# Later weight requests, a value matrix in one piece and a quantised matrix cast on GpSimd: a change to the first chunks of an attention-and-gate kernel

## The chip, the cores and the metric

The kernel runs on the 8 cores of one Trainium2 chip. Each core gets two of the 16 sequences and its own copy of the weights; the cores exchange nothing. The metric is the device time of the slowest core, in microseconds (us), as a median of 3 runs. A profile of one execution, taken on the slowest core, goes with it.

## What is computed

Per core x is 4096 x 1024 in float32. The reference, cut to what matters:

```python
xn = _layernorm(x, axis=-1)
q, k, v = xn @ Wq.T, xn @ Wk.T, xn @ Wv.T       # 16 heads of 64
scores = q k^T / 8, each query sees itself and the 127 keys before it
s = softmax(scores) @ v @ Wo.T
q_lhs = round(xn / (max|xn| per row / 127)); q_rhs = round(rhs / (max|rhs| per column / 127))
g = silu((q_lhs @ q_rhs) * lhs_scale * rhs_scale)
x + s * g
```

## The kernel before, in words

The 4096 rows are cut into 32 chunks of 128 rows. Names: `xs` (four buffers) holds a chunk of x as it lands, `xnr` its normalised bf16 form and `xnt` its transpose; `qlr` and `qlt` are the same for the quantised rows. `qrhs` is the quantised right-hand matrix, `rsb` its column scales. `wq`, `wk`, `wv`, `wo` are the weights in bf16, each asked for as 8 row blocks, which GpSimd's DMA queue casts from float32 on the way (`load_w`). rhs comes from SyncE's queue in 8 blocks (`load_rh`, called rh0 to rh7 here).

Every engine has its program written out by hand, and waits on counters of the others. PE's order is `pe_order`: a list of groups. TX, TL, TR, TA are transposes on PE (of `xnr`, `qlr`, of a cast rhs block, of the attention output); Q, K, V, O are the projections; F is the quantised product; RS spreads the column scales over the partitions; S and A are scores and attention-times-V of a quarter of the heads. A group name has an index (chunk, pair of chunks or block) and a half. `slot_gaps(c)` gives the groups that PE does between the four score blocks b = 0 to 3 of chunk c; "slot (c,b)" below is the stretch after score block b of chunk c. VectorE and ScalarE walk the same list: `evac_v` and `evac_a` empty the PSUM banks, in the order of the slots, and the table `extra` puts other work into a slot. A PSUM bank is filled again four groups later, so a late evacuation stops PE.

The start-up before chunk 0 runs: x of chunks 0 to 3 arrives; VectorE takes mean and variance (`bn`), GpSimd the reciprocal root (`rstd`), VectorE writes `xnr` (`xn`), PE transposes it (TX). ScalarE centres (`cen`) and scales (`qp`), VectorE takes the row maximum (`amax`) and finishes the quantised row (`ql`). PE does Q, K and V of chunks 0 to 3, then TL, TR 0 to 3 and RS. A rhs block goes through five steps: `rabs` (VectorE, maximum of the block), `rscale` (VectorE, once for two blocks), `rq` (ScalarE, scale and round), `rcast` (GpSimd, to bf16), TR (PE). In the steps of V the eight row blocks of `wv` are consumed in the order in which they arrive: first blocks 0 to 3 for all eight groups, then blocks 4 to 7 group by group. The gate of chunk c is `zev` (VectorE, F out of PSUM), tanh (`th`, ScalarE), `gate` (VectorE).

SyncE asks for x of chunks 0 to 3 at once, for rh0 to rh3 when block 4 of `wk` has landed, for x 4 and 5 when block 2 of `wv` has, and for rh4 to rh7 and x 6 when block 6 has. GpSimd asks for `wv` when rh1 has landed.

## Time and profile before

| | |
|---|---|
| median of 3 runs | 712.0 us (710.03 to 713.23) |
| the profiled execution | 712.11 us |
| its span on the slowest core | 710.5 us (the cores: 703.9 to 710.5 us) |
| PE busy | 665.4 us, 94% of the span |
| VectorE / ScalarE / GpSimd busy | 67% / 49% / 24% |
| granted TensorE clock, mean of the core | 0.985 |

The span runs from the first to the last instruction of that core; 1.6 us of the execution's time lie around it. Busy PE is not PE at its peak: a wait shows as idle time, and a low clock as longer busy time. The granted clock of a stretch is a share of full speed, 1.00 being 2.4 GHz and 0.50 being 1.2 GHz.

### The profile page before, as it was taken

To read this page: it belongs to the slowest core of one execution; us is meant where nothing else is said; L and a number is where in the kernel's file an instruction comes from. 1 tells how busy PE (TensorE), PEld (TensorE's weight loads), DVE (VectorE), ACT (ScalarE), POOL (GpSimd) and SP (SyncE) were. 2 spreads that over 40 slices of the span, in tenths; PEclk is the share of its full clock that TensorE was granted. 3 is DMA by queue.
4 is the path that set the end of the run, shared out by engine and by line. 5 is a ranking of instruction groups with operands and counts; after the bars stand their busy time and mean duration, and the time that the engine had idled before them with its cause. 6 is when DMAs were issued, how large, how long until landed. Compare 5 with 4: busy or idle time off the path is not lost.

```text
span 710.5 us, 17009 instructions; the slowest of 8 cores (703.9 to 710.5 us)
## 1 busy us (share of the span) xinstructions
PE 665.4 (94%) x5724; PEld 413.0 (58%) x5724; DVE 475.9 (67%) x958; ACT 346.7 (49%) x473; POOL 172.6 (24%) x281
## 2 busy tenths in 40 slices
...
GB/s 191 149 200 188 182 18 76 149 119 134 134 129 127 119 88 97 131 120 134 134 120 127 115 102 94 130 120 134 135 122 125 115 92 104 131 89 76 76 90 149
DMA packets 109859, 86.40 MB, mean 122 GB/s; under 512 B 92112, under 2 KB 92240, under 8 KB 109776
## 3 DMA queue, kind: packets, MB, share of 16 engines
...
q8 instruction: 49, 0.80, 0.5%
...
## 4 chain that ended last, share of the span: by engine, by line
PE 87%; DVE 5%; DMA 4%; issue 2%; POOL 1%; ACT 1%; DVEq 0%; SPq 0%; ACTq 0%; POOLq 0%
PE pj L675 44%; PE pj L666 29%; PE psc L759 5%; PE pav L783 4%; PE pav L785 2%; DMA xs<-x 2%; DMA wv<-wvt 2%; DVE ee L356 1%; PE pav L666 1%; PE psc L666 1%; DVE sm L326 1%; DVE gg L385 0%; DVE sm L291 0%; DVE sm L403 0%; POOL aot L831 0%
## 5 line engine op out<-in xcount | busy, mean ns | idle before, releaser
L573 ACT ACTIVATE ee<-psc 128x1024 bf16<-128x1024 f32 (+1 forms) x128 | 128.4, 1003 | 157.8 <-PE psc L759 152.9
L825 POOL TENSOR_TENSOR xr<-tt,xr 128x512 f32<-128x512 f32 x63 | 80.4, 1277 | 370.0 <-DVE tt L391 344.6
L675 PE MATMUL pj<-wv,xnt 128*128 128x512 bf16 x480 | 118.7, 391 | 5.1 <-DMA wv<-wvt 3.8
L675 PE MATMUL pj<-qrhs,qlt 128*128 128x512 bf16 x512 | 122.0, 382 | 0.0
L675 PE MATMUL pj<-wo,aot 128*128 128x512 bf16 x512 | 116.4, 379 | 1.2 <-ACT aot L313 1.2
L666 PE MATMUL pj<-xnt,wq 128*128 128x256 bf16 x960 | 112.3, 276 | 1.9 <-DVE xnt L311 1.8
L666 PE MATMUL pj<-xnt,wk 128*128 128x256 bf16 x960 | 109.7, 273 | 0.0
L356 DVE TENSOR_TENSOR ee<-ee,mask_s 128x1024 bf16<-128x1024 bf16 (+1 forms) x128 | 104.1, 813 | 7.6 <-ACT ee L573 2.1
L666 PEld LDWEIGHTS pj<-xnt,wq 128*128 128x128 bf16 x960 | 93.1, 99 | 13.5 <-issue 2.1
L666 PEld LDWEIGHTS pj<-xnt,wk 128*128 128x128 bf16 x960 | 92.0, 98 | 10.3
L675 PEld LDWEIGHTS pj<-wo,aot 128*128 128x128 bf16 x512 | 49.5, 98 | 60.0 <-issue 1.7
L391 DVE TENSOR_TENSOR tt<-pj,gg 128x512 f32<-128x512 f32 x64 | 44.0, 690 | 54.4 <-PE pj L675 53.4
L675 PEld LDWEIGHTS pj<-qrhs,qlt 128*128 128x128 bf16 x512 | 48.3, 99 | 54.3 <-issue 2.8
L675 PEld LDWEIGHTS pj<-wv,xnt 128*128 128x128 bf16 x480 | 45.9, 100 | 53.1 <-issue 12.0
L539 ACT ACTIVATE xs<-xs,sm 128x1024 f32<-128x1024 f32 x32 | 36.6, 1148 | 75.5 <-DVE xnr L321 75.5
L367 DVE TENSOR_TENSOR ao<-pav,sm 128x256 bf16<-128x256 f32 x128 | 54.4, 425 | 13.3
L326 DVE TENSOR_REDUCE sm<-xs 128x1 f32<-128x1024 f32 x32 | 39.0, 1218 | 34.9 <-ACT xs L539 34.9
L759 PEld LDWEIGHTS psc<-qt,kt 64*128 64x128 bf16 x992 | 28.1, 94 | 49.6 <-issue 49.4
L378 DVE SCALAR_TENSOR_TENSOR zz<-pj,sm,rsb 128x512 f32<-128x512 f32 x64 | 47.8, 747 | 10.7 <-PE pj L675 7.8
L759 PE MATMUL psc<-qt,kt 64*128 64x128 bf16 x992 | 50.1, 219 | 2.5 <-ACT ee L573 2.5
L783 PE MATMUL pav<-vv,ee 128*128 128x65 bf16 x480 | 46.5, 196 | 6.0 <-DVE ee L356 3.4
L556 ACT CAST kt<-pj 128x512 bf16<-128x512 f32 x60 | 33.6, 582 | 32.2 <-PE pj L666 32.2
...
## 6 DMA issues: line engine op xcount, KB each, us to landing
...
```

The source lines that it names most:

```text
L326: op(lambda: v.reduce_max(col(c, AMAX), xs[c % XS][:], AX.X, apply_absolute_value=True), "v")
L356: op(lambda: v.tensor_tensor(a, a, m, ALU.mult), "v", ("mask", c, b))
L367: op(lambda: v.tensor_tensor(view(ao[c % 2], b * 256, (64, 4), (1, 64)), view(p, 0, (66, 4), (1, 64)), bass.AP(sm, C_RS + 4 * (b % 2), [[1 ...
L378: op(lambda: v.scalar_tensor_tensor(zz[h], banks[bank["F", c, h]], col(c, LSH), rsb[:, h * 512:(h + 1) * 512], ALU.mult, ALU.mult), "v", ( ...
L391: op(lambda: v.tensor_tensor(tt[h], banks[bank["O", c, h]], gg[c % 2][:, h * 512:(h + 1) * 512], ALU.mult), "v", ("ev", "O", c, h))
L539: op(lambda: a.activation(xs[c % XS][:], xs[c % XS][:], AF.Identity, scale=-1.0, bias=col(c, MEAN)), "a", ("cen", c))
L573: op(lambda: a.activation(o, i, AF.Exp, scale=0.125), "a", ("exp", c, b))
L666: yield [(lambda kc=kc, m=m: t.matmul(p[:, m * 256:(m + 1) * 256], w[:, kc * 1024 + (2 * j + m) * 128:kc * 1024 + (2 * j + m + 1) * 128], ...
L675: yield [lambda kc=kc: t.matmul(p[:], src[:, off + kc * step:off + kc * step + 128], w[:, kc * 1024 + j * 512:kc * 1024 + (j + 1) * 512], ...
L759: todo.append(lambda m=m, kk=kk, ko=ko, rows=rows, q0=q0: t.matmul(psc[:, q0:q0 + 128], kk[rows, m * 256 + ko:m * 256 + ko + 128], qt[s % ...
L783: todo.append(lambda out=out, e0=e0, vp=vp: t.matmul(out, e[:, e0:e0 + 128], vp, start=True, stop=False))
L825: op(lambda: p.tensor_tensor(r, tt[h], r, ALU.add), "p", ("add", c, h))
```

## The change

Six edits. GpSimd asks for the first block of `wq` only when the statistics of chunk 0 are done; the remaining requests follow in other portions. All 8 blocks of `wv` are asked for in one go, ahead of the casts of rhs blocks 0 to 3; SyncE asks for x 4 and 5 behind block 6 of `wv`. Blocks 4 to 7 of rhs are scaled and rounded on GpSimd (`rq_p`) and not on ScalarE, and two blocks of `wo` go ahead of them, six in between. ScalarE empties both halves of TX and TR from index 4 on. The orders of the start-up and of chunks 0 to 3 change on every engine: F of chunks 0 and 1 stands in the slots of chunk 0, TX 4 and 5 at the end of chunk 0, and VectorE's work on chunks 4 and 5 and on rhs 4 to 7 behind the first mask. In chunks 2 and 3 SyncE's transposes stand ahead of its stores. At the end the last transpose stands between the two halves of the last O.

```diff
@@ slot_gaps
     if c == 0:
-        return [halves("TX", 4, 5), halves("V", 4)[:1], halves("V", 4)[1:], []]
+        return [[("F", 0, 0)], [("F", 1, 0)] + halves("TR", 4), halves("TR", 5), halves("TX", 4, 5)]
     if c == 1:
-        v, f1 = halves("V", 5), [("F", i, 1) for i in range(2)]
-        return [halves("TR", 4, 5), v[:1] + halves("TR", 6, 7), v[1:] + [("RS", 0, 1)] + f1[:1], f1[1:]]
+        v4, v5 = [[g] for g in halves("V", 4)], [[g] for g in halves("V", 5)]
+        return [v4[0] + halves("TR", 6, 7), v4[1] + [("RS", 0, 1)], v5[0] + [("F", 0, 1)], v5[1] + [("F", 1, 1)]]
@@ pe_order
-    out = one(halves("TX", 0, 1)) + [("G", q0, range(4))] + one(halves("TX", 2)) + [("G", q0, range(4, 5))]
-    out += one(halves("TX", 3)) + [("G", q1, range(5)), ("G", q0, range(5, 6)), ("G", q1, range(5, 6))]
+    out = one(halves("TX", 0, 1)) + [("G", q0, range(6))] + one(halves("TX", 2, 3)) + [("G", q1, range(6))]
...
-    out += one(halves("TL", 2, 3) + halves("TR", 0, 1, 2, 3) + [("RS", 0, 0), ("F", 0, 0), ("F", 1, 0)])
+    out += one(halves("TL", 2, 3) + halves("TR", 0, 1, 2, 3) + [("RS", 0, 0)])
...
-    out += [("G", [g], range(6)) for g in last] + one([("TA", NC - 1, 3)])
+    out += [("G", last[:1], range(6))] + one([("TA", NC - 1, 3)]) + [("G", last[1:], range(6))]
     out += [("G", [g], range(6, 8)) for g in last]
@@ evacuator
+    if k in ("TX", "TR") and i >= 4:
+        return "a"
@@ emit_sync
-            landed(sync, "wv2", 0)
+            landed(sync, "wv6", 0)
             load_x(sync, 4)
             load_x(sync, 5)
-            landed(sync, "wv6", 0)
             for i in range(4, 8):
                 load_rh(sync, i)
...
-                if c >= 2:
+                if c in (2, 3):
+                    t_ql(sync, c + 2)
+                elif c >= 4:
                     store(sync, c - 2)
...
+                if c in (2, 3):
+                    store(sync, c - 2)
@@ emit_vector
             evac_v(v, ("TX", 0, 0))
+            evac_v(v, ("TX", 1, 0))
             bn(v, 3)
-            evac_v(v, ("TX", 1, 0))
...
+            extra = {(0, 0): [(bn, 4), (bn, 5), (rabs, 4), (rabs, 5), (rscale, 4)], (0, 1): [(rabs, 6)], (0, 2): [(xn, 4), (xn, 5)],
+                     (0, 3): [(rabs, 7), (rscale, 6)], (1, 0): [(rdiag, 1)], (1, 2): [(amax, 4)],
+                     (2, 0): [(ql, 4)], (2, 2): [(amax, 5)], (3, 0): [(ql, 5)]}
@@ emit_scalar
-            extra = {(0, 1): [(rq, 6)], (0, 2): [(rq, 7)], (1, 0): [(qp, 4)], (1, 3): [(qp, 5)]}
+            extra = {(1, 0): [(cen, 4)], (1, 2): [(cen, 5)],
+                     (1, 3): [(qp, 4)], (2, 3): [(qp, 5)]}
@@ GpSimd
+        def rq_p(p, i):
+            need(p, "v", ("rsc", i - i % 2))
+            st = stage[i]
+            op(lambda: p.tensor_scalar(st[:], st[:], sm[:, C_RSC + i:C_RSC + i + 1], MAGIC, ALU.mult, ALU.add),
+               "p", ("rq", i))
@@ emit_gpsimd
+            need(p, "v", ("bn", 0))
             load_w(p, 0, range(2))
-            need(p, "v", ("bn", 0))
-            load_w(p, 0, range(2, 4))
             rstd(p, 0)
-            load_w(p, 0, range(4, 8))
+            load_w(p, 0, range(2, 6))
             rstd(p, 2)
+            load_w(p, 0, range(6, 8))
             load_w(p, 1, range(8))
             landed(p, "rh1", 0)
-            load_w(p, 2, range(4))
-            rcast(p, 0)
-            rcast(p, 1)
-            load_w(p, 2, range(4, 8))
-            rcast(p, 2)
-            rcast(p, 3)
+            load_w(p, 2, range(8))
+            for i in range(4):
+                rcast(p, i)
+            landed(p, "rh4", 0)
+            load_w(p, 3, range(2))
+            for i in (4, 5):
+                rq_p(p, i)
+                rcast(p, i)
             rstd(p, 4)
-            landed(p, "rh6", 0)
-            load_w(p, 3, range(8))
-            for i in range(4, 8):
+            load_w(p, 3, range(2, 8))
+            for i in (6, 7):
+                rq_p(p, i)
                 rcast(p, i)
```

GpSimd's queue from the second block of `wv` on (L831 and L828 are `rcast`, L818 is `rq_p`; `sm` rows are `rstd`). Before:

```order
L837 DMA wv<-wvt 128x1024 x3
L831 TENSOR_SCALAR aot<-gg 128x1024 [waits s_a] x2
L837 DMA wv<-wvt 128x1024 x4
L831 TENSOR_SCALAR ao<-zz 128x1024 [waits s_a]
L831 TENSOR_SCALAR ao<-tt 128x1024 [waits s_a]
L808 TENSOR_SCALAR sm<-sm 128x2 [waits s_v]
L810 TENSOR_TENSOR sm<-sm 128x2 [waits s_p]
L812 TENSOR_TENSOR sm<-sm 128x2 [waits s_p]
L814 TENSOR_TENSOR sm<-sm 128x2 [waits s_p]
L816 TENSOR_SCALAR sm<-sm 128x2 [waits s_p]
L818 TENSOR_TENSOR sm<-sm 128x2 [waits s_p]
L837 DMA wo<-wot 128x1024 [waits s_rh6]
```

With the change:

```order
L834 DMA wv<-wvt 128x1024 x7
L828 TENSOR_SCALAR aot<-gg 128x1024 [waits s_a] x2
L828 TENSOR_SCALAR ao<-zz 128x1024 [waits s_a]
L828 TENSOR_SCALAR ao<-tt 128x1024 [waits s_a]
L834 DMA wo<-wot 128x1024 [waits s_rh4]
L834 DMA wo<-wot 128x1024
L818 TENSOR_SCALAR xr<-xr,sm 128x1024 [waits s_v]
L828 TENSOR_SCALAR aot<-xr 128x1024 [waits s_p,s_t]
L818 TENSOR_SCALAR xr<-xr,sm 128x1024 [waits s_v]
L828 TENSOR_SCALAR aot<-xr 128x1024 [waits s_p,s_t]
L796 TENSOR_SCALAR sm<-sm 128x2 [waits s_v]
L798 TENSOR_TENSOR sm<-sm 128x2 [waits s_p]
```

The requests for `wv` stand together, and the requests for `wo` are split around two pairs of `rq_p` and `rcast`; `rstd` of chunks 4 and 5 has moved behind them.

VectorE behind the evacuation of TR 0 to 3 (L403 and L407 are `rabs`, the four short rows behind two of them `rscale`). Before:

```order
L321 TENSOR_SCALAR xnr<-xs,sm 128x1024 [waits s_p,s_t] x2
L403 TENSOR_REDUCE sm<-xr 128x1 [waits s_rh4]
L378 SCALAR_TENSOR_TENSOR zz<-pj,sm,rsb 128x512 [waits s_t,s_a,s_p]
L403 TENSOR_REDUCE sm<-xr 128x1 [waits s_rh5]
L409 TENSOR_SCALAR sm<-sm 128x2 [waits s_v]
L411 RECIPROCAL sm<-sm 128x2 [waits s_v]
L412 TENSOR_SCALAR sm<-sm 128x2
L414 TENSOR_SCALAR sm<-sm 128x2 [waits s_v]
L385 SCALAR_TENSOR_TENSOR gg<-gg,zz 128x512 [waits s_a]
L378 SCALAR_TENSOR_TENSOR zz<-pj,sm,rsb 128x512 [waits s_t,s_v]
L403 TENSOR_REDUCE sm<-xr 128x1 [waits s_rh6]
L385 SCALAR_TENSOR_TENSOR gg<-gg,zz 128x512 [waits s_a]
```

With the change (`rscale`'s last row and `zz`, the evacuation of F of chunk 0, come next):

```order
L360 TENSOR_TENSOR ee<-ee,mask_s 128x4x128 [waits s_a,s_lm]
L295 BN_STATS sm<-xs 128x6 [waits s_lx0]
L295 BN_STATS sm<-xs 128x6
L297 BN_AGGR sm<-sm 128x2 [waits s_v]
L295 BN_STATS sm<-xs 128x6 [waits s_lx1]
L295 BN_STATS sm<-xs 128x6
L297 BN_AGGR sm<-sm 128x2 [waits s_v]
L407 TENSOR_REDUCE sm<-xr 128x1 [waits s_rh4]
L407 TENSOR_REDUCE sm<-xr 128x1 [waits s_rh5]
L413 TENSOR_SCALAR sm<-sm 128x2 [waits s_v]
L415 RECIPROCAL sm<-sm 128x2 [waits s_v]
L416 TENSOR_SCALAR sm<-sm 128x2
```

The mask of the first score block stands first, and the statistics of chunks 4 and 5 and two block maxima lie between it and the first `zz`.

PE at the same place, behind RS (`qrhs,qlt` is F, `qt,kt` S, `vv,ee` A, `ident_s,xnr` TX and `ident_s,aot` TR). Before:

```order
L675 MATMUL pj<-qrhs,qlt 128x512 [waits s_a,s_v]
L675 MATMUL pj<-qrhs,qlt 128x512 x7
L675 MATMUL pj<-qrhs,qlt 128x512 [waits s_a,s_v]
L675 MATMUL pj<-qrhs,qlt 128x512 x7
L759 MATMUL psc<-qt,kt 128x128 [waits s_a,s_v]
L759 MATMUL psc<-qt,kt 128x128 x3
L660 MATMUL pj<-ident_s,xnr 128x128 [waits s_a,s_v]
L660 MATMUL pj<-ident_s,xnr 128x128 x3
L660 MATMUL pj<-ident_s,xnr 128x128 [waits s_a]
L660 MATMUL pj<-ident_s,xnr 128x128 x3
L660 MATMUL pj<-ident_s,xnr 128x128 [waits s_v]
```

With the change:

```order
L747 MATMUL psc<-qt,kt 128x128 [waits s_a,s_v]
L747 MATMUL psc<-qt,kt 128x128 x3
L663 MATMUL pj<-qrhs,qlt 128x512 [waits s_a,s_v]
L663 MATMUL pj<-qrhs,qlt 128x512 x7
L747 MATMUL psc<-qt,kt 128x128 [waits s_a]
L747 MATMUL psc<-qt,kt 128x128 x3
L773 MATMUL pav<-vv,ee 128x65 [waits s_v,s_a]
L773 MATMUL pav<-vv,ee 128x65 x3
L663 MATMUL pj<-qrhs,qlt 128x512 [waits s_a,s_v]
L663 MATMUL pj<-qrhs,qlt 128x512 x7
L648 MATMUL pj<-ident_s,aot 128x128 [waits s_a,s_p]
```

The first score block has moved ahead of F, and TR 4 stands where TX 4 and 5 stood.

## Rows read from the trace of the kernel before

**Rows 1.** Busy time in stretches: us, each engine's busy (instructions), granted clock, DMA share, GB/s.

```profile
20.00:38.00 18.00, 15.74 (x138) 13.37 (x137) 10.14 (x26) 8.01 (x11) 5.47 (x10) 1.00 1.04 153
64.30:71.50 7.20, 5.88 (x15) 2.03 (x16) 1.49 (x3) 1.74 (x3) 1.69 (x6) 0.53 0.82 211
230.00:650.00 420.00, 420.00 (x3663) 261.68 (x3662) 291.46 (x580) 213.95 (x293) 98.84 (x162) 1.00 0.54 117
```

**Rows 2.** Waits of PE: what waited for whom, us in total, times, longest.

```profile
PE pj L660 <- DVE xnr L321: 14.9, 1, 14.9
PE pj L660 <- DVE zz L378: 4.6, 1, 4.6
PE pj L675 <- DMA wv<-wvt: 3.8, 3, 2.5
PE pav L783 <- DVE ee L356: 3.4, 4, 1.3
```

**Rows 3.** Timeline of PE: start, us, operation, out<-in, count, idle before and releaser.

```profile
18.63 5.88 PE L666 MATMUL pj<-xnt,wq 128*128 128x256 bf16 x32 [1.85 <-DVE xnt L311]
...
28.53 0.60 PE L666 MATMUL pav<-xnt,wq 128*128 128x256 bf16 x4 [2.25 <-DVE xnt L311]
...
54.34 3.80 PE L675 MATMUL pj<-wv,xnt 128*128 128x512 bf16 x16 [1.17 <-DVE qlt L311]
...
66.79 5.04 PE L675 MATMUL pj<-wv,xnt 128*128 128x512 bf16 x13 [0.66 <-DMA wv<-wvt]
...
79.80 3.62 PE L675 MATMUL pj<-qrhs,qlt 128*128 128x512 bf16 x16
...
91.58 3.51 PE L675 MATMUL pj<-wv,xnt 128*128 128x512 bf16 x8
...
115.94 0.40 PE L759 MATMUL psc<-qt,kt 64*128 64x128 bf16 x8
```

**Rows 4.** Timeline of all engines, 0 to 30 us.

```profile
5.03 1.29 DVE L291 BATCH_NORM_STATS2 sm<-xs 128x6 f32<-128x512 f32 x2 [3.21 <-DMA xs<-x]
...
12.30 0.20 POOL L818 TENSOR_TENSOR sm<-sm 128x2 f32<-128x2 f32 x1
...
16.46 1.28 DVE L291 BATCH_NORM_STATS2 sm<-xs 128x6 f32<-128x512 f32 x2 [0.43 <-DMA xs<-x]
...
24.84 0.42 DVE L311 COPY xnt<-pav 128x512 bf16<-128x512 bf16 x1 [2.46 <-PE pav L660]
```

**Rows 5.** Timeline of all engines, 43 to 66 us.

```profile
43.59 2.11 POOL L837 DMA_DIRECT2D wv<-wvt  x4 [17.61 <-DMA gg<-rhst]
...
52.68 2.35 POOL L837 DMA_DIRECT2D wv<-wvt  x4
...
65.47 0.80 SPq L252 DMA_DIRECT2D xr<-rhst  x2
```

**Rows 6.** Timeline of all engines, 79 to 93 us.

```profile
80.05 0.59 ACT L589 COPY rsb<-pav 128x512 f32<-128x512 f32 x1 [0.47 <-PE pav L655]
...
82.61 1.21 DVE L403 TENSOR_REDUCE sm<-xr 128x1 f32<-128x1024 f32 x1
...
84.75 0.17 DVE L414 TENSOR_SCALAR sm<-sm 128x2 f32<-128x2 f32 x1
...
86.38 1.04 POOL L831 TENSOR_SCALAR aot<-xr 128x1024 bf16<-128x1024 f32 x1 [7.42 <-ACT xr L550]
...
86.79 1.18 DVE L385 SCALAR_TENSOR_TENSOR gg<-gg,zz 128x512 f32<-128x512 f32 x1 [1.87 <-ACT gg L579]
...
90.88 0.62 ACT L573 ACTIVATE ee<-psc 128x512 bf16<-128x512 f32 x1
```

**Rows 7.** Timeline of all engines, 699 to 711 us.

```profile
700.04 1.26 POOL L825 TENSOR_TENSOR xr<-tt,xr 128x512 f32<-128x512 f32 x1 [1.29 <-DVE tt L391]
...
700.67 2.75 PE L675 MATMUL pj<-wo,aot 128*128 128x512 bf16 x12 [0.61 <-ACT aot L313]
...
704.14 1.02 PE L675 MATMUL pj<-wo,aot 128*128 128x512 bf16 x4 [0.61 <-ACT aot L313]
```

27 lines of the change are left out of this document (5 added, 22 removed).

## The prediction

> **What bounds the kernel now.** I read the busy time in stretches first. From 230 to 650 us PE is busy for 420.00 of 420.00 us at full clock [rows 1], and the change touches nothing there; so only the ends can give time. The waits of PE come next: 14.9 us until the first normalised chunk, 4.6 us for a bank that `zz` had not left, 3.8 us for blocks of `wv`, 3.4 us for masks [rows 2]. In the timeline of PE [rows 3] the reader is to see a ladder of starts: Q at 18.63, the second Q half at 28.53, V at 54.34, the last 29 V products from 66.79, F at 79.80, V of chunk 4 at 91.58 and the first score block of chunk 2 at 115.94. I follow the change to that last mark and carry the difference over, since PE alone sets the pace behind it. A 512-column product takes 0.22 us (16 in 3.62 us from 79.80, less the 0.16 us that the last one outlasts its slot), twice that at the half clock (8 in 3.51 us from 91.58, granted clock 0.50 to 0.53 in such stretches [rows 1, 3]); a 256-column product takes 0.11 us. The sum is made against the profiled execution's 712.11 us, which is the median's 712.0 within 0.1.
>
> **First chunks.** Before, x of chunk 3 landed only at 16.46, because the `wq` blocks shared the DMA engines, and PE's first transpose waited for `xn` at 14.92, which stood behind the statistics of chunk 2 [rows 3, 4]. With the requests held back, statistics run without a pause: chunk 0 from 5.03 to 6.6, then 1.6 us each, so 8.2, 9.8. GpSimd's `rstd` ended 12.50 before, 2.7 us behind the statistics of chunk 1 [rows 4]: now 8.2 + 2.7 = 10.9. `xn` takes 0.8, so PE starts at 11.7, 3.2 us earlier. Q started 3.7 us after the first transpose before (14.92 to 18.63 [rows 3]), 0.5 of it behind the fourth chunk's statistics, which now come later, but ScalarE's copy, centring, copy keeps nearly all: 15.2.
> The first 32 Q products took 5.88 us, the start at low speed; then 16 more take 1.8: TX 2 and 3 start at 22.8 (before 24.3). What is late next is the second Q half: VectorE copies one transpose, does `ql` and `amax`, and copies the other; before, this ran from 24.84 until Q went on at 28.53, 3.7 us [rows 3, 4]. PE had 8 products to put under it, now none. Copy at 23.3, Q at 27.0, with PE idle for 3.1 us instead of 2.3. Then 80 Q products and not 88 (8.7 us) and 128 of K (14.0) lead to 49.7, TL and the wait behind it take 2.3 as before: V at 52.0, 2.3 us earlier than 54.34. The weights don't stop this: `wq` blocks 2 to 5 are asked for from 10.9 to 13.8, and a block moves in 1.7 us (0.262 MB at 153 GB/s, DMA share 1.04 [rows 1]), so block 5 is there at some 20, two steps ahead. The DMA engines are full in 20 to 38 us before; what x gains at the front the weights lose, so `wk` and rh1 land when they did, and `wv` is asked for at 43.6 as before [rows 5].
>
> **V.** Before, blocks 4 to 7 were asked for at 52.68, behind two casts that waited for ScalarE, and shared the engines with x 4 and 5, asked for at 52.72 when block 2 had landed [rows 5]; the last block let PE go on at 66.79, and the clock fell to 0.53 of full speed for 7 us [rows 1, 3]. Now all eight follow one another. Block 2 lands at 52.7 again and five more need 5 x 1.7 = 8.6: the last is there at 61.3. If the fourth block was already through by 53, it is 60.0; at 2 us a block, 62.7. Behind it stand 29 products, 6.3 us: V ends at 67.6 (bounds 66.3 and 69.0; PE alone, 52.0 + 64 x 0.22, asks for 65.9). Before it ended at 66.79 + 4.9 + 16 x 0.22 = 75.1. **Gain at this mark 7.5 us.** x 4 and 5 and rh4 to rh7 are asked for at some 60 instead of 52.7 and 65.5 [rows 5]: seven transfers of 512 KB, done by about 74, which the statistics of chunk 4 (67.6 + 7.2) just don't wait for. Casts 0 to 3 move behind the last `wv` request, at some 48, and are done by 59; TR needs them at 69. They cost nothing while V covers them.
>
> **Chunks 0 and 1**, counted from the end of V, T. TL, TR and RS take 4.7 (75.1 to 79.80 [rows 3]). The score block needs the bank of RS, which ScalarE emptied at 80.64, T+5.5 [rows 6]; F used to cover that wait, and PE now stands still for 0.9. Score block T+5.6, exponential 0.6 [rows 6], and 0.7 for the mask with its wake-up: T+7.2. Then VectorE does two statistics (3.1), two block maxima (1.2 each) and `rscale` (1.0, by 83.83 to 84.92 [rows 6]): T+13.6. GpSimd's `rq_p` is in no row. Its nearest is the cast of the same tile with one input, 1.04 us [rows 6]; the two-input addition of 512 columns, 1.26 [rows 7], would make it 2.5; ScalarE's loss of the work gives PE nothing. I take 1.04, since input and size are the cast's: TR 4 can start at T+13.6 + 0.1 + 1.04 + 0.15 + 1.04 = T+16.0. PE has F, S, A and F until T+9.8. **New wait 6.2 us**, and the clock will fall in it, as it did around the 4.6 us before. TR 5 follows at T+18.2; `rstd` of chunks 4 and 5 (2.5) and `xn` (0.8) come behind it, TX at T+21.7, masks and copies, V of chunk 4 at T+23.7. Before it was at T+16.5 (91.58), but with TR 4 and 5 and two F halves' worth of waits still ahead. At half clock V ends at T+27.2. GpSimd asks for six `wo` blocks (3.3), waits for `rscale` 6 (T+25.5) and does two pairs of 2.25: TR 6 T+28.0, TR 7 T+30.2. Behind them PE has 5 groups of 8 products (8.7), RS (0.9) and score work (1.7): T+42.0, and 0.6 for clock: T+42.6. Before it was 115.94 - 75.1 = T+40.8. **Loss 1.8 us.** The mark is at 67.6 + 42.6 = 110.2 instead of 115.9: 5.7 us earlier.
> One rule speaks against GpSimd here. The gate at 86.79 took 1.18 us and not the 0.68 of others of its kind beside the cast of 86.38 to 87.42 [rows 6]: it held back until the cast was through. The Trainium skill says the same in SBUF — State Buffer, Who interferes with whom: a VectorE instruction with two SBUF inputs and a GpSimd one that reads SBUF exclude each other for a whole instruction. By the row each of eight GpSimd steps can hold a mask or gate back by up to 1 us; nearly all of that lies while PE waits for the cast anyway. I count 0, upper bound 1.5.
>
> **Chunks 2 and 3, and the end.** The transposes ahead of the stores cost SyncE nothing that PE sees. `amax` 5 (2.1 us with its short steps) enters slot (2,2) and `ql` 5 slot (3,0); both lie under 3.5 us or more of products. The mask waits (3.4 us [rows 2]) fall mostly in chunk 3, behind `rstd` and centring, and stay: 0, bounds -3 and +1. At the end 12 O products, a transpose, a copy and 4 products ran from 700.67 to the last start at 704.14 and behind it [rows 7]; with the transpose between the halves, six products cover the copy, so the last four start at 703.4: gain 0.7.
> Sum: 712.1 - 5.7 - 0.7 = **705.7 us**.
>
> **The rivals.**
> (a) The new waits let the clock fall. PE idles 3.1 us ahead of Q, up to 2.5 in pieces in V, 6.2 in chunk 0. A fall at Q costs 4 us of work at half speed, 2 us; one in V another 2. For: behind the wait of 2.5 us for `wv` it stood at 0.53 [rows 1, 2]. Against: behind the 2.3 us ahead of 28.53 four products took 0.60, full speed [rows 3]. Time 709.5.
> The Trainium skill (TensorE: Matmul & The Clock Gate, What's actually happening) calls half speed the default that only activity lifts, which fits the slow first 32 Q products.
> (b) Slower: GpSimd becomes the bound of chunks 0 and 1. With `rq_p` at 2.5 us each pair takes 3.7 instead of 2.25: TR 5 and `rstd` 3.0 later, TR 7 4.5 later, 1.5 for the exclusions, 2 for clock: 713.7. It decides above about 4 us a pair, or 3.5 with low clock. Against: the cast's row.
> (c) More is won: the mask waits of chunk 3 go with the new order and the last `wv` block is there at 60: 701.7.
> (d) `wv` comes no sooner, since the DMA engines were full anyway. For: their share is near 1 throughout. Against: x 4 and 5 are 1 MB that now comes after. Time 709, with (a).
>
> **How the numbers follow.** The forecast 0.55 (703 to 708.3), (a) and (d) 0.23, (b) 0.07, (c) 0.15. A measurement of this kernel tells about 0.5%, 3.6 us, from no change. Faster than 708.4: the forecast and (c), 0.70; slower than 715.6: half of (b) and some for mechanisms unseen, 0.06; within: 0.24. The range reaches into (c) and over (a): 701.5 to 711.
>
> **What would show it.** PE's first transpose near 11.7 and V near 52; no wait for `wv` above 2 us and TL at 66 to 69; then the longest wait of PE behind the start at TR 4, some 6 us, released by GpSimd; `rq_p` near 1.04 us; chunk 2's first score block at 109 to 112. Wrong would be: `wv` landing after 64, PE at half clock for most of 27 to 52, or a pair on GpSimd above 3.5 us.

## The result

The changed kernel takes 714.8 us (median), the kernel before 712.0 us. The ratio is 1.0043, with a 95% interval of 1.0031 to 1.0056: the change makes this kernel slower by 0.4%, some 3 us, where 705.7 us and a gain of 6.3 us were forecast. The measured time also lies outside the range of 701.5 to 711.0 us. Single executions of either kernel were sometimes disturbed and much longer; the ratios leave these out.

The profiled execution of the changed kernel has its slowest core at 713.3 us. Spans and granted clock of the cores, then PE's waits on core 7, the slowest (what waited for whom, us in total, times, longest):

```profile
core 4: 713.2 us, clock 0.981
core 5: 711.4 us, clock 0.979
core 6: 709.5 us, clock 0.983
core 7: 713.3 us, clock 0.981
```

```profile
PE pj L648 <- DVE xnr L325: 18.7, 2, 16.9
PE pj L648 <- POOL aot L828: 9.6, 4, 5.8
PE pav L771 <- DVE ee L360: 4.4, 5, 1.3
PE pav L654 <- DVE xnt L315: 3.1, 1, 3.1
PE pj L654 <- ACT xnt L317: 1.5, 1, 1.5
```

Against [rows 2] the wait for `wv` (3.8 us) is gone: that part of the change does what it says. In its place stand 9.6 us behind GpSimd's casts (`aot`, L828) and 3.1 us instead of 2.3 ahead of the second Q half, and the first transpose is 2 us later (16.9 us on this core, 14.9 on the slowest one before). The ladder of PE's starts, to be laid beside [rows 3]:

```profile
20.23 6.87 PE L654 MATMUL pj<-xnt,wq 128*128 128x256 bf16 x48 [1.49 <-ACT xnt L317]
...
31.13 1.01 PE L654 MATMUL pav<-xnt,wq 128*128 128x256 bf16 x4 [3.14 <-DVE xnt L315]
...
58.87 3.37 PE L663 MATMUL pj<-wv,xnt 128*128 128x512 bf16 x14 [1.17 <-DVE qlt L315]
...
72.86 0.61 PE L648 MATMUL pav<-ident_s,qlr 128*128 128x128 bf16 x8
...
89.20 1.01 PE L648 MATMUL pj<-ident_s,aot 128*128 128x128 bf16 x8 [5.78 <-POOL aot L828]
...
98.31 3.60 PE L663 MATMUL pj<-wv,xnt 128*128 128x512 bf16 x8
...
118.59 0.40 PE L747 MATMUL psc<-qt,kt 64*128 64x128 bf16 x8
```

V ends at 72.86 (75.1 before), but the first score block of chunk 2 starts at 118.59 (115.94 before). Between the two the changed kernel spends 45.7 us and the kernel before 40.8. The clock says the same. Busy time in stretches of core 7 (columns as in [rows 1]):

```profile
26.00:40.00 14.00, 10.86 (x83) 8.52 (x81) 7.37 (x19) 4.33 (x6) 3.12 (x6) 0.76 1.07 152
58.90:72.90 14.00, 13.97 (x65) 6.29 (x66) 3.53 (x8) 6.32 (x9) 2.19 (x3) 1.00 0.82 217
85.00:95.00 10.00, 3.35 (x32) 2.29 (x32) 7.49 (x17) 4.42 (x8) 6.83 (x11) 0.66 0.00 1
95.00:105.00 10.00, 6.79 (x45) 3.76 (x46) 7.05 (x14) 5.68 (x9) 8.48 (x10) 0.66 0.77 115
150.00:160.00 10.00, 7.63 (x41) 3.30 (x40) 6.78 (x16) 3.77 (x5) 0.40 (x1) 0.83 0.33 91
```

V runs at full speed without a gap. From 85 to 95 us PE works for 3.35 of 10 us while VectorE and GpSimd are busy for 7.5 and 6.8: PE waits for their preparation, not for data (DMA share 0.00).

One core is not enough to read such small shifts, because the cores differ. The table gives medians over the eight cores of one profiled execution of each kernel: PE's first transpose, start of the second Q half, of K and of V, V's end (T), from there to V of chunk 4 and to the first score block of chunk 2 (S20), and from the first Q product in chunk 2 to the first in chunk 4 ("Q to Q", which holds chunks 2 and 3). All in us. The runs were made on several chips, on which the kernel before took 709.9 to 712.7 us; the ratio is always that of the times to the kernel before on the same chip, with its interval.

```
kernel            TX    Q2    K     V     T     T>V4  T>S20 Q to Q  ratio (interval)
before            15.2  28.1  39.1  55.4  74.3  16.5  40.8  39.1    1
after             14.1  29.7  40.1  56.4  70.5  25.5  46.8  41.6    1.0043 (1.0031 to 1.0056)
e1_early_w        15.3  30.2  40.5  56.8  70.7  25.5  46.9  41.5    1.0029 (1.0014 to 1.0044)
e2_late_w         14.1  27.1  37.7  54.0  75.4  16.5  40.8  39.0    1.0004 (0.9986 to 1.0022)
e3_rq_scalar      14.3  29.8  39.3  55.7  70.4  24.6  41.6  41.3    0.9961 (0.9944 to 0.9978)
e4_scales_first   14.6  30.0  40.4  56.6  70.7  20.0  40.4  41.5    0.9964 (0.9940 to 0.9987)
e5_start_order    14.1  27.6  37.3  53.5  69.2  25.5  45.9  41.4    1.0029 (1.0013 to 1.0045)
e6_wv_alone       15.7  28.9  39.6  55.8  69.8  21.9  46.7  39.0    1.0000 (0.9986 to 1.0013)
e7_e3_and_e4      14.0  29.3  38.9  55.3  70.0  20.3  37.2  40.5    0.9907 (0.9886 to 0.9928)
e8_rows45_early   14.2  29.4  39.5  55.7  69.7  25.5  45.9  39.1    1.0011 (1.0001 to 1.0021)
e9_four_parts     14.0  27.1  37.2  53.5  68.4  20.3  37.2  39.3    0.9889 (0.9868 to 0.9910)
e10_covers        14.4  27.1  37.7  54.0  68.8  20.4  37.8  37.0    0.9886 (0.9855 to 0.9918)
e11_five_parts    13.9  27.5  37.3  53.6  68.4  20.3  37.2  37.0    0.9852 (0.9829 to 0.9876)
e12_chunk3_alone  15.0  28.5  38.3  54.5  71.9  16.4  39.6  36.8    0.9966 (0.9955 to 0.9977)
```

The last row tells how well these marks repeat, since up to chunk 3 that kernel is the kernel before: its V ends at 71.9 us and not 74.3, and it needs 39.6 us and not 40.8 from T to S20, while T to V of chunk 4 agrees within 0.1. So a mark counted from the start of the program wanders by 2 to 3 us between two executions, and a stretch behind T by about 1.

By the first two rows the change wins 3.8 us at T (1.4 against the last row), loses 6.0 between T and S20, and loses another 2.5 in chunks 2 and 3. The end gives 0.6 us back: from the first Q of chunk 6 to the end of the span 513.03 us before (710.5 - 197.47, core 5) and 512.46 now (713.3 - 200.84, core 7).

### The profile page after: what moved, and what is told of

It is laid out like the page before. It is cut to its first block, busy times and chain, and to the rows that moved or that the text cites. A ratio compares the mean times of both kernels' runs of the same rounds, so it can differ in the third digit from the quotient of the medians.

```text
span 713.3 us, 17008 instructions; the slowest of 8 cores (709.2 to 713.3 us)
## 1 busy us (share of the span) xinstructions
PE 666.2 (93%) x5724; PEld 414.6 (58%) x5724; DVE 475.1 (67%) x952; ACT 346.2 (49%) x475; POOL 176.4 (25%) x285
## 4 chain that ended last, share of the span: by engine, by line
PE 85%; DVE 6%; issue 4%; POOL 2%; DMA 1%; ACT 1%; DVEq 0%; POOLq 0%; SPq 0%; ACTq 0%
PE pj L663 42%; PE pj L654 28%; PE psc L747 5%; PE pav L771 4%; PE pav L773 2%; DMA xs<-x 1%; DVE ee L360 1%; PE pav L654 1%; PE psc L654 1%; DVE sm L295 1%; DVE sm L330 1%; DVE sm L407 0%; DVE tt L395 0%; PE psc L663 0%; PE pav L663 0%
## 5 line engine op out<-in xcount | busy, mean ns | idle before, releaser
L663 PE MATMUL pj<-wv,xnt 128*128 128x512 bf16 x480 | 115.9, 386 | 1.2 <-DVE qlt L315 1.2
L360 DVE TENSOR_TENSOR ee<-ee,mask_s 128x1024 bf16<-128x1024 bf16 (+1 forms) x128 | 107.0, 836 | 9.2 <-ACT ee L566 4.1
L663 PEld LDWEIGHTS pj<-wv,xnt 128*128 128x128 bf16 x480 | 45.6, 99 | 46.8 <-issue 4.6
L549 ACT CAST qt<-pj 128x512 bf16<-128x512 f32 x60 | 33.4, 584 | 33.6 <-PE pj L654 33.6
```

The source lines that it names most:

```text
L360: op(lambda: v.tensor_tensor(a, a, m, ALU.mult), "v", ("mask", c, b))
L663: yield [lambda kc=kc: t.matmul(p[:], src[:, off + kc * step:off + kc * step + 128], w[:, kc * 1024 + j * 512:kc * 1024 + (j + 1) * 512], ...
```

## The experiments

**Are the late weight requests the cause?** The first run takes them back, the second makes them alone in the kernel before.

```diff
+            load_w(p, 0, range(2))
             need(p, "v", ("bn", 0))
-            load_w(p, 0, range(2))
+            load_w(p, 0, range(2, 4))
             rstd(p, 0)
-            load_w(p, 0, range(2, 6))
+            load_w(p, 0, range(4, 8))
             rstd(p, 2)
-            load_w(p, 0, range(6, 8))
```

> The changed kernel with one part undone: GpSimd asks for the blocks of wq as the kernel before did (blocks 0 and 1 at once, 2 and 3 behind the statistics of chunk 0, 4 to 7 behind the first rstd). All else stays. Theory: the late requests idle the DMA engines for some 5 us at the front, which is paid back as late wk and rh1, a late wv request (43 to 49.5 us over the cores) and a start of V at 54.6 to 58.9 us; and they carry the spread of x's arrival through to the end. Then V starts at 53.5 to 55.5 on all cores, the first score block of chunk 2 moves from 115.1 to 118.6 us down to 114 to 116, and the time falls by 2 to 3.5 us below the changed kernel's 714.8: 711.3 to 712.8, ratio to the kernel before about 1.000. Rival (the wait of 3.1 us ahead of the second Q half and its low clock set V's start, whenever the blocks come): V at 54.6 to 58 as now, time within 1 us of 714.8.

> The kernel before with one part of the change alone: the late requests for wq (nothing before the statistics of chunk 0, then 2 blocks, rstd, 4 blocks, rstd, 2 blocks). Theory (late requests cost on the slowest core): PE's first transpose 1 to 2 us earlier, the wv request up to 4 us later on the cores where x comes late, V starting at 55 to 58.5, time 2 to 3 us above the kernel before: ratio 1.003 to 1.004. Rival (the start of V is bounded by PE's own work, as the prediction had it): V 1 to 2 us earlier, ratio 0.997 to 0.999.

My theory fell in both. With the early requests the changed kernel starts V at 56.8 us as with the late ones (56.4), and its time is the same within the two intervals. In the kernel before, the late requests go with a V that starts 1.4 us earlier (55.4 to 54.0), as the rival said, though 54.5 was also seen without them (e12); but `wv` is then asked for at 46.3 us instead of 43.5 (medians of the cores), V ends at 75.4 instead of 74.3, and the ratio is 1.0004. No gain or loss of the requests shows in the time either way: what x gains, the last weights lose.

**What does PE wait for in chunk 0?** Two runs on two suspects, each a part of the new order. In the first, ScalarE scales and rounds blocks 4 to 7 again:

```diff
-            extra = {(1, 0): [(cen, 4)], (1, 2): [(cen, 5)],
+            extra = {(1, 0): [(rq, 6), (rq, 7), (cen, 4)], (1, 2): [(cen, 5)],
...
                     ex(a, c, b)
+                    if (c, b) == (0, 1):
+                        rq(a, 4)
+                        rq(a, 5)
...
             for i in (4, 5):
-                rq_p(p, i)
                 rcast(p, i)
```

> The changed kernel with scale-and-round of rhs 4 to 7 back on ScalarE (4 and 5 behind the second exponential, 6 and 7 behind the first of chunk 1); places on the other engines unchanged. Theory (GpSimd's pair of steps is on the path: 1.11 to 1.80 us each on four blocks, PE waits behind TR 4, TR 5 and TR 7): TR 4 within 0.3 us of where it is, TR 5 and V of chunk 4 2 to 2.5 us earlier, TR 7 2 us earlier, time 3 to 4 us below 714.8. Rival (VectorE's chain of statistics, maxima and scales behind the first mask is what PE waits for, GpSimd's steps are a small part): time within 1.5 us of 714.8, since TR 4 stays and ScalarE's exponentials and tanh come up to 1 us later.

In the second, VectorE takes the maxima of rhs 4 and 5 before the first mask:

```diff
             for i in range(4):
                 evac_v(v, ("TR", i, 0))
-            extra = {(0, 0): [(bn, 4), (bn, 5), (rabs, 4), (rabs, 5), (rscale, 4)], (0, 1): [(rabs, 6)], (0, 2): [(xn, 4), (xn, 5)],
+            rabs(v, 4)
+            rabs(v, 5)
+            rscale(v, 4)
+            extra = {(0, 0): [(bn, 4), (bn, 5)], (0, 1): [(rabs, 6)], (0, 2): [(xn, 4), (xn, 5)],
```

> The changed kernel with three of VectorE's steps moved: the maxima of rhs 4 and 5 and their scale (rabs, rabs, rscale) stand ahead of the first mask, where VectorE idles for 3.15 us, instead of behind the statistics of chunks 4 and 5. Theory (the chain that starts behind the first mask bounds chunk 0): the scale is there 6 us earlier, TR 4 starts at 10 to 11 us behind the end of V instead of 16.3 and its wait of 5.8 us goes to under 1; then TX of chunk 4 waits for rstd and is 5 to 7 us earlier, V of chunk 4 at 18 to 20 instead of 25.5, the clock stays up, and the first score block of chunk 2 comes 5 to 7 us earlier: time 708 to 710. Rival (GpSimd's queue, with six weight requests and four pairs of steps, bounds it): TR 4 earlier, but TX, TR 6 and TR 7 within 2 us of where they are, time 713 to 714.

Both mechanisms held, and the first was sized wrong. Without `rq_p` TR 4 stays at T + 16.3 and T to S20 falls from 46.8 to 41.6 us; the ratio falls by 0.0082, or 5.8 us, where 3 to 4 us had been expected. V of chunk 4 is only 0.9 us earlier and not 2 to 2.5; the start of TR 7 moves by 2.6 us (T + 32.1 to T + 29.5), and from there to S20 it is 12.1 us instead of 14.7. The waits of PE in T to S20 fall by 3.3 us of the 5.2; the rest is faster work, so the clock. With the scales first TR 4 starts at T + 10.4 instead of 16.3, V of chunk 4 at 20.0 instead of 25.5, T to S20 is 40.4 us; the ratio falls by 0.0079. The rows show both mechanisms. All engines of the changed kernel, core 7, from 79 us:

```profile
79.95 0.42 DVE L360 TENSOR_TENSOR ee<-ee,mask_s 128x512 bf16<-128x512 bf16 x1 [3.15 <-ACT ee L566]
80.30 1.28 DVE L295 BATCH_NORM_STATS2 sm<-xs 128x6 f32<-128x512 f32 x2
...
83.30 2.32 DVE L407 TENSOR_REDUCE sm<-xr 128x1 f32<-128x1024 f32 x2
...
86.33 0.17 DVE L418 TENSOR_SCALAR sm<-sm 128x2 f32<-128x2 f32 x1
86.68 1.11 POOL L818 TENSOR_SCALAR xr<-xr,sm 128x1024 f32<-128x1024 f32 x1 [12.79 <-DVE sm L418]
...
88.01 1.04 POOL L828 TENSOR_SCALAR aot<-xr 128x1024 bf16<-128x1024 f32 x1 [0.22 <-POOL xr L818]
88.23 1.09 DVE L360 TENSOR_TENSOR ee<-ee,mask_s 128x512 bf16<-128x512 bf16 x1
89.03 1.80 POOL L818 TENSOR_SCALAR xr<-xr,sm 128x1024 f32<-128x1024 f32 x1
...
101.06 1.52 DVE L424 TENSOR_TENSOR rsb<-ident_s,sm 128x512 f32<-128x512 bf16 x1
102.03 1.54 POOL L818 TENSOR_SCALAR tt<-tt,sm 128x1024 f32<-128x1024 f32 x1
```

VectorE idles 3.15 us until the mask at 79.95 and only then starts statistics and maxima; the scale is ready at 86.5 and GpSimd, idle for 12.79 us, begins. One after the other come two scalings and two casts on one engine. The mask at 88.23 takes 1.09 us instead of 0.42 beside the cast, and the next scaling takes 1.80 us instead of 1.11. The Trainium skill names the reason in SBUF — State Buffer, Who interferes with whom: a VectorE instruction with two SBUF inputs and a GpSimd one that reads SBUF hold each other off. The trace agrees with these numbers. The write of `rsb` at 101.06 and the scaling at 102.03 belong to the second pair of blocks: the first runs beside a cast (100.82 to 102.04) and the scaling, and both are drawn out.

**Are these two waits or one?** Both edits together:

> The changed kernel with both edits of the last two: scale-and-round of rhs 4 to 7 on ScalarE, and the maxima and scale of rhs 4 and 5 ahead of the first mask. Each alone took 5 us (714.8 to 709.9 and 710.2). Theory (two separate waits: VectorE's chain ahead of TR 4 and GpSimd's pairs ahead of TR 5, TX and TR 7): the sum is nearly kept; TR 4 at 10.4 us behind V's end, V of chunk 4 at 18 to 19, first score block of chunk 2 at 36.5 to 38.5 behind V's end (changed kernel 46.8, the two edits 41.6 and 40.3); time 706 to 708. Rival (both gave back the same time, the clock that falls in a wait of some 6 us and stays low for 20 us): 39.5 to 41, time 709 to 710.

They are two, with 2 us in common. T to S20 is 37.2 us, 9.6 below the changed kernel where the single edits took 5.2 and 6.4, and the time is 705.5 us. With the scales early, GpSimd's steps cost 3.2 us (40.4 to 37.2). TR 4 starts at T + 11.7 and not at the 10.4 expected, since ScalarE takes up the scaling only behind its second exponential, and V of chunk 4 at T + 20.3 and not 18 to 19; the gain comes behind them. All engines on core 3 of that kernel, its slowest:

```profile
75.92 2.33 DVE L407 TENSOR_REDUCE sm<-xr 128x1 f32<-128x1024 f32 x2
...
79.16 0.43 DVE L360 TENSOR_TENSOR ee<-ee,mask_s 128x512 bf16<-128x512 bf16 x1
...
81.25 2.17 ACT L546 ACTIVATE xr<-xr,sm 128x1024 f32<-128x1024 f32 x2
...
82.61 2.07 POOL L831 TENSOR_SCALAR aot<-xr 128x1024 bf16<-128x1024 f32 x2 [7.76 <-PE pj L669]
...
83.80 0.61 PE L654 MATMUL pj<-ident_s,aot 128*128 128x128 bf16 x8 [1.18 <-POOL aot L831]
...
94.47 0.69 DVE L424 TENSOR_TENSOR rsb<-ident_s,sm 128x512 f32<-128x512 bf16 x1
```

The maxima fill the hole ahead of the mask and cost the mask nothing, and ScalarE scales while GpSimd casts: PE's wait ahead of TR 4 is 1.18 us and no longer 5.78. VectorE's write of `rsb` takes 0.69 us here and took 1.52 in the changed kernel, beside GpSimd's cast and scaling.

**What does the order of the start-up cost?** The changed kernel with TX 2, four Q products, TX 3 and the copies in the order of before:

```diff
-    out = one(halves("TX", 0, 1)) + [("G", q0, range(6))] + one(halves("TX", 2, 3)) + [("G", q1, range(6))]
+    out = one(halves("TX", 0, 1)) + [("G", q0, range(4))] + one(halves("TX", 2)) + [("G", q0, range(4, 5))]
+    out += one(halves("TX", 3)) + [("G", q1, range(5)), ("G", q0, range(5, 6)), ("G", q1, range(5, 6))]
...
-            evac_v(v, ("TX", 1, 0))
             bn(v, 3)
+            evac_v(v, ("TX", 1, 0))
```

> The changed kernel with the start-up order of before on PE and VectorE (TX 2, four more Q products, TX 3; statistics of chunk 3 between the two copies of TX 0 and TX 1); requests, wv and chunks 0 to 3 stay as changed. Theory (the new order of the Q steps leaves one wait of 3.1 us with nothing under it and lets the clock fall to 0.76 from 26 to 40 us): over the cores the second Q half moves from 29.6 us to 27 to 28, K from 40.2 to 37.5 to 38, V's start from 56.6 to 54 to 54.5, clock 0.95 or more from 26 to 40; V then waits 1 to 2 us for blocks of wv, so that V ends 1 to 2 us earlier than 70.9; time 713 to 714, 1 to 2 us below the changed kernel. Rival (wv's arrival sets V's end anyway): V ends at 70.5 to 71.5 as now and the time stays at 714.5 to 715. Second rival (V is bound by nothing but its own start): V ends 2.6 us earlier, time 712.

The marks came as the theory had them: second Q half 27.6 us, K 37.3, V 53.5, T 69.2 instead of 70.5. The ratio falls by 0.0014, or 1 us, which lies within the two intervals; the marks show it, the times alone would not. PE's rows behind the wait, on core 7 of the changed kernel and on core 0 of this one:

```profile
33.64 1.06 PE L654 MATMUL psc<-xnt,wq 128*128 128x256 bf16 x4
```

```profile
26.48 0.60 PE L655 MATMUL pav<-xnt,wq 128*128 128x256 bf16 x4 [2.25 <-DVE xnt L316]
26.92 0.60 PE L655 MATMUL psc<-xnt,wq 128*128 128x256 bf16 x4
```

and the second one's busy time in the stretch that has clock 0.76 on core 7 of the changed kernel, 0.88 on the other seven:

```profile
26.00:40.00 14.00, 13.52 (x124) 12.15 (x125) 6.94 (x16) 5.33 (x8) 0.00 (x0) 1.00 0.99 164
```

Behind the wait of 3.14 us groups of four products start 0.85 us apart, behind this wait of 2.25 us 0.44 us apart: the wait is 0.9 us longer, and the half clock behind it costs K another 1.7 us (second Q half to K 10.4 us instead of 8.7 forecast).

But core 0 here is a good core, and so is the one that [rows 3] shows. On core 0 of the kernel before the same wait is followed by the half clock:

```profile
27.63 0.60 PE L666 MATMUL pav<-xnt,wq 128*128 128x256 bf16 x4 [2.26 <-DVE xnt L311]
...
28.79 1.06 PE L666 MATMUL pav<-xnt,wq 128*128 128x256 bf16 x4
```

From the second Q half to K the kernel before takes 11.3 us on six of its eight cores and 9.6 on two (3 and 5); this kernel takes 11.3 on two cores and 9.6 on six, with the same products and the same wait. Of the 2.9 us that V gains here, up to 1.7 on a core is that luck of the clock. What the order itself shows is a wait shorter by 0.9 us with eight products done ahead of it.

**Is `wv` in one piece worth what I gave it?** That part alone in the kernel before, with the statistics of chunks 4 and 5 behind the copies of TR so that VectorE doesn't stand still for x 4 and 5:

```diff
-            landed(sync, "wv2", 0)
+            landed(sync, "wv6", 0)
             load_x(sync, 4)
             load_x(sync, 5)
-            landed(sync, "wv6", 0)
...
-            bn(v, 4)
-            bn(v, 5)
             evac_v(v, ("TL", 2, 0))
             evac_v(v, ("TL", 3, 0))
             for i in range(4):
                 evac_v(v, ("TR", i, 0))
+            bn(v, 4)
+            bn(v, 5)
...
-            load_w(p, 2, range(4))
+            load_w(p, 2, range(8))
             rcast(p, 0)
             rcast(p, 1)
-            load_w(p, 2, range(4, 8))
```

> The kernel before with one part alone: wv asked for in one piece ahead of the casts, x 4 and 5 asked for behind block 6 of wv, and, so that VectorE doesn't stand still for them, the statistics of chunks 4 and 5 behind its copies of TR 0 to 3. Theory (this part is worth what it was meant for): no wait for wv above 1 us, V ends at 69.5 to 71 instead of 74.3 (median of the cores), the rest follows with 0 to 2 us lost to the later statistics; time 709 to 710.5, 2 to 3.5 below the kernel before. Rival (V's end is set by the DMA engines in either order): V ends at 73 to 75, time 712 to 714.

The first half of the theory held, the second fell. V ends at 69.8 us instead of 74.3 (71.9 in e12), and the ratio is 1.0000. S20 is at 116.4 us (median) against 115.2. PE on core 7, behind F of chunk 0:

```profile
75.31 3.62 PE L674 MATMUL pj<-qrhs,qlt 128*128 128x512 bf16 x16
...
81.28 0.96 PE L659 MATMUL pj<-ident_s,xnr 128*128 128x128 bf16 x8 [2.14 <-DVE xnr L320]
83.90 0.58 PE L659 MATMUL pj<-ident_s,xnr 128*128 128x128 bf16 x4 [1.66 <-DVE zz L377]
89.93 0.59 PE L659 MATMUL pj<-ident_s,xnr 128*128 128x128 bf16 x4 [5.45 <-DVE zz L377]
```

In the kernel before, VectorE and GpSimd did the statistics and `rstd` of chunks 4 and 5 under V (on core 5 from 59.65 to 68.6 us). In this kernel the work stands behind V's end, and PE waits there for `rstd` and `xn` and for the evacuation of F queued behind them (`zz`), 9.3 us in three pieces, where [rows 2] has one such wait of 4.6 us. That is the price of these steps behind V. It isn't the price of `wv` in one piece, because the edit itself put them there, behind the copies of TR. The same core:

```profile
60.45 0.90 SPq L208 DMA_DIRECT2D xs<-x  x2
...
71.12 0.42 DVE L310 COPY qlt<-pav 128x512 bf16<-128x512 bf16 x1 [10.43 <-PE pav L659]
...
74.48 1.28 DVE L290 BATCH_NORM_STATS2 sm<-xs 128x6 f32<-128x512 f32 x2
```

x 4 and 5 landed 6.0 and 7.3 us after they were asked for, by 68.2 us at the latest; VectorE idled until 71.12 and took their statistics at 74.48. So they could have been taken some 6 us earlier, and no run did that: what `wv` in one piece is worth with them in that hole stays open.

**What happens in chunks 2 and 3?** The changed kernel with the rows of chunks 4 and 5 quantised earlier, in gaps of VectorE (ScalarE's centring of chunk 5 and its scaling of chunks 4 and 5 move up, too):

```diff
-                     (0, 3): [(rabs, 7), (rscale, 6)], (1, 0): [(rdiag, 1)], (1, 2): [(amax, 4)],
-                     (2, 0): [(ql, 4)], (2, 2): [(amax, 5)], (3, 0): [(ql, 5)]}
+                     (0, 3): [(rabs, 7), (rscale, 6)], (1, 0): [(rdiag, 1)], (1, 1): [(amax, 4)], (1, 2): [(amax, 5)], (1, 3): [(ql, 4)],
+                     (2, 0): [(ql, 5)]}
```

> The changed kernel with the rows of chunks 4 and 5 quantised earlier: amax 4, amax 5 and ql 4 in slots (1,1), (1,2), (1,3), ql 5 in (2,0), ScalarE's centring and scaling of chunk 5 one and four slots earlier; nothing of the rest of chunks 0 and 1 moves. Before, from the first Q of chunk 2 to the next Q took 39.1 us on six cores and 40.6 on two; in the changed kernel it takes 41.5 on six. Theory (amax 5 in slot (2,2) delays VectorE's answer to PE, adds a wait of 0.6 us there and the clock falls in chunk 3): back to 39.1 to 40.6 us, the wait of 0.64 us ahead of O in chunk 2 gone, time 713 to 713.8. Rival (chunk 3's own chain of rstd, xn, centring and amax makes the waits and the clock falls by chance): 41.5 on most cores as now, time 714.5 to 715.

The theory held: Q to Q is 39.1 us again (the median; 40.8 on three cores), the ratio falls by 0.0032, or 2.3 us. I had put `amax` 5 and `ql` 5 down as free, "under 3.5 us or more of products". The wait that is there in both kernels, in chunk 3, grew by 0.2 us (PE, core 5 before and core 7 after):

```profile
147.93 0.40 PE L759 MATMUL psc<-qt,kt 64*128 64x128 bf16 x8 [0.82 <-ACT ee L573]
```

```profile
151.22 0.40 PE L747 MATMUL psc<-qt,kt 64*128 64x128 bf16 x8 [1.05 <-ACT ee L566]
```

Together with 0.6 us in chunk 2 this is 0.9 us. The rest, 1.6 us, is the clock, which fell in that place on two of eight cores before (Q to Q 40.6 and 40.7 us there, 39.1 on the others) and on seven of eight after (41.3 to 41.6, and 39.9 on the eighth).

**Do the four parts add, and what is left?** The two edits of chunk 0, the start-up order and the rows of chunks 4 and 5 together; then three covers more (F of chunk 0 ahead of the first score block, the maximum of rhs 6 behind `xn`, and in chunk 3 `cen`, `amax`, `qp` and `ql` of chunk 7 later):

```diff
-        return [[("F", 0, 0)], [("F", 1, 0)] + halves("TR", 4), halves("TR", 5), halves("TX", 4, 5)]
+        return [[("F", 1, 0)], halves("TR", 4), halves("TR", 5), halves("TX", 4, 5)]
...
-    out += one(halves("TL", 2, 3) + halves("TR", 0, 1, 2, 3) + [("RS", 0, 0)])
+    out += one(halves("TL", 2, 3) + halves("TR", 0, 1, 2, 3) + [("RS", 0, 0), ("F", 0, 0)])
...
-                    if ln and b == 1:
+                    if ln and b == 1 + (c == 3):
                         cen(a, c + 4)
```

> The changed kernel with all four edits that each took time off: maxima and scale of rhs 4 and 5 ahead of the first mask, scale-and-round on ScalarE, the start-up order of before, and the rows of chunks 4 and 5 quantised earlier. The first two together ran at 705.65 us; the start-up order alone took 0.8 us and chunks 2 and 3 alone 1.9 us off the changed kernel's 714.8. Theory (the four places are separate and their prices add): V starts at 53.5 and ends at 68.5 to 69.5 us, first score block of chunk 2 at 36 to 37.5 behind that, from Q of chunk 2 to the next Q 39 to 39.5 us instead of 40.5; time 702.5 to 704. Rival (what is won in one place is waited for in the next): 705 to 706.

> The last kernel with work laid over three waits that are left: F of chunk 0 back ahead of the first score block (1.1 us wait for the bank of RS), the maximum of rhs 6 behind xn of chunks 4 and 5 instead of ahead of the evacuation of F of chunk 1 (1.8 us wait in TR 5), and in chunk 3 the centring, maximum and scaling of chunk 7 one to three slots later (waits of 1.05 and 1.3 us for exponential and mask, with a fall of the clock on some cores). Theory: first score block of chunk 2 at 34.5 to 35.5 behind the end of V, from Q of chunk 2 to the next Q 37.0 to 37.5 us (PE alone), time 699 to 701. Rival (the chain of rstd behind the statistics sets TX and V of chunk 4 whatever stands ahead): 36 to 37 behind V, only chunk 3 gains, time 701 to 703.

The four parts add in the marks: V, T to S20 and Q to Q each have, within 0.2 us, the value that their own edits gave. In the ratio they give 0.0154, or 11 us, of 0.0207 that the single ones sum to, so in the time they overlap by a quarter, as far as intervals of 0.002 to either side can tell. Of the three covers the one in chunk 3 did what it should: Q to Q is 37.0 us. The other two together did harm: T to S20 is 37.8 us instead of 37.2. Three stretches of core 2 of that kernel show why:

```profile
80.00:85.00 5.00, 1.63 (x18) 1.07 (x16) 4.42 (x10) 2.82 (x4) 2.74 (x4) 0.71 0.13 25
85.00:90.00 5.00, 3.67 (x36) 3.04 (x36) 4.87 (x10) 4.33 (x9) 4.17 (x9) 0.50 0.00 0
90.00:95.00 5.00, 4.50 (x22) 1.61 (x20) 4.32 (x13) 3.95 (x6) 1.68 (x4) 0.50 1.03 134
```

The wait of 1.1 us for the bank was gone, but the work that covered the next wait had been used up, so that one grew from 1.2 to 2.9 us, and the clock stood at 0.50 from 85 to 95; with the four parts it stood at 0.50 from 85 to 90 and at 0.94 from 90 to 95 on that core. Which of the two covers did it wasn't separated. So the last kernel keeps chunk 3's cover alone, and the kernel before gets it, too:

```diff
-                     (2, 0): [(ql, 5)]}
+                     (2, 0): [(ql, 5)], (3, 3): [(amax, 7)], (4, 0): [(ql, 7)]}
...
-                        amax(v, c + 4)
-                    if ln and b == 2:
+                        if c != 3:
+                            amax(v, c + 4)
+                    if ln and b == 2 and c != 3:
```

> The kernel of the four edits and, of the three covers, chunk 3's alone (centring, maximum and scaling of chunk 7 one to three slots later). F of chunk 0 stays behind the first score block: putting it ahead had made one wait of 2.9 us out of two short ones, with the clock at 0.50 from 85 to 95 us, and the first score block of chunk 2 came 0.6 us later behind V. Theory: behind V's end 37.2 us to that block as with the four edits, from Q of chunk 2 to the next Q 37.0 us instead of 39.3; time 2.3 us below 703.5: 700.8 to 702. Rival (the slowest core is set by when x arrives, and the gain goes in that spread): 702 to 703.5.

> The kernel before with that edit of chunk 3 alone. There the stretch from Q of chunk 2 to the next Q takes 39.1 us on most cores and 40.6 where the clock falls. Theory (its two waits of 0.8 and 1.3 us, and the fall of the clock, come from chunk 7's centring and maximum standing ahead of ScalarE's evacuation of K and VectorE's mask): 37.0 us on all cores, time 2 us below the kernel before: 709.5 to 710.5, ratio 0.996 to 0.998. Rival (the waits belong to the masks and tanh of chunk 3 itself): 38 to 39, time within 0.7 us of the kernel before.

Both held in their marks. The last version has ratio 0.9852, 10.5 us below the kernel before; its profiled execution took 698.8 us, below the 700.8 to 702 expected, but on a chip where the kernel before is faster, too (709.9 us, and 711.2 beside the four parts). The edit of chunk 3 alone gives 0.9966 (2.4 us): Q to Q 36.8 us on all eight cores, which is PE's own work. It has nothing to do with the change that was studied, and is the surest gain in it: two waits of 0.8 and 1.3 us in an otherwise gapless stretch. The last kernel's slowest core, and chunks 2 and 3 on it:

```profile
core 5: 697.3 us, clock 0.988
```

```profile
112.00:150.00 38.00, 37.69 (x347) 24.32 (x346) 29.80 (x61) 19.47 (x25) 14.22 (x20) 1.00 0.49 110
```

## Why the prediction was wrong, step by step

Three terms of the sum failed: V was put at 52.0 and started at 56.4 us (2.4 us of it in the first transpose, 1.7 in the clock behind the wait ahead of Q); "Loss 1.8 us" for chunks 0 and 1 was 6.0; and chunks 2 and 3, put at 0, cost 2.5.

**First transpose, 11.7 us.** Wrong by 2.4 us in the median (14.1; 12.9 to 16.9 over the cores). "With the requests held back, statistics run without a pause" failed. On core 7 x of chunk 0 is there at 7.10 and that of chunk 1 only at 11.52:

```profile
7.10 1.28 DVE L295 BATCH_NORM_STATS2 sm<-xs 128x6 f32<-128x512 f32 x2 [5.27 <-DMA xs<-x]
...
11.52 1.29 DVE L295 BATCH_NORM_STATS2 sm<-xs 128x6 f32<-128x512 f32 x2 [2.83 <-DMA xs<-x]
```

GpSimd's first request for `wq` on this core came at 9.31, so until then nothing but the other x transfers and two small ones was beside it. On all eight cores the statistics of chunk 1 start 2.6 to 4.4 us behind those of chunk 0, where 1.6 was forecast; before, with the requests early, it was 1.5 to 3.3. The sum also took the one start of [rows 4], 5.03 us, for all cores, where it is 4.6 to 7.6 us over the cores of the two kernels; the time is that of the slowest core.

**Wait ahead of the second Q half.** The wait was right (3.1 forecast, 3.14 measured). That the clock holds was wrong: rival (a) came true here, for 1.7 us. I had taken the 2.25 us wait of [rows 3] as the evidence against it, though the new one is longer, and though that core is one of only two on which the clock held; on the other six cores before it fell behind the same wait (11.3 us from the second Q half to K instead of 9.6). From the first transpose to V, 42.3 us instead of 40.3: V at 56.4 instead of 52.0.

**V.** The mechanism was right and the duration better than forecast: 14.0 us, PE's own work, instead of 15.6. T came out at 70.5 instead of 67.6, all of it from the late start. The gain at T was also overstated by the base: 75.1 us is the slowest core's, the median of the cores before is 74.3. Gain 3.8 us, not 7.5, and less still if the 71.9 of e12 is taken for the kernel before.

**Chunks 0 and 1, "Loss 1.8 us".** The mechanism was right: the statistics behind T were counted, the casts cost nothing under V, and TR 4 came at T + 16.3 where T + 16.0 was forecast. The sum was still 4.2 us too small: 1.9 of it is there at TR 7 (T + 32.1, forecast 30.2), 2.3 come behind it. V of chunk 4 came at 25.5 instead of 23.7: `rq_p` takes 1.11 us, 1.54 to 1.80 beside VectorE's two-input work, where 1.04 was taken. Rival (b)'s mechanism was real, though at a quarter of its price (1.39 us in the mean of the four, not 2.5). A pair took 2.7 us, far below the 4, or 3.5 with low clock, from which on it was to decide; yet the steps on GpSimd cost 5.2 us (e3), because they delay everything behind them and hold the clock down. And the clock term, 0.6 us, was mis-sized most: at 0.66 from 85 to 105 us, V of chunk 4's second half and RS ran slow too.

**The exclusions, "I count 0".** On core 7 the mask lost 0.67 us and `rq_p` 0.69 and 0.43; the e3 run removes them with the step, so their own share isn't settled.

**Chunks 2 and 3, 0 with bounds -3 and +1.** Wrong at 2.5 us, outside the bound (e8).

**The end, 0.7.** Right: 0.6 by the spans.

In the forecast's own sum: 5.7 us earlier at S20 became 2.1 later (front 4.4, chunks 0 and 1 4.2, less 1.5 in V, and 0.7 because S20 before is 115.2 in the median and not 115.9); chunks 2 and 3 added 2.5; the end gave 0.6. That makes 4.0 by medians of cores, and 2.8 between the slowest ones (713.3 - 710.5), since the slowest core before was one of the two that already paid the clock in chunk 3. With four misplaced steps put right the kernel has ratio 0.9889, 7.9 us below the kernel before, so the order of the steps took back more than was forecast as gain. How much of those 7.9 us comes from `wv` in one piece isn't shown; no run takes that part alone out of it. Faster had a chance of 0.70 because each rival was priced alone; here (a) at Q and (b) in part came together, with chunk 3, whose cost no rival named.
